# One list schedule for all engines, built groups by turns in two places of PSUM, and the dense unit of 181 nodes first

## The reference

```python
def gnn(features, src, dst, edge_weight, W, b):
    msgs = features[src] * edge_weight[:, None]
    agg = jax.ops.segment_sum(msgs, dst, num_segments=3125, indices_are_sorted=True)
    return jnp.einsum('ni,oi->no', agg, W) + b

def ffn(x, ...):                      # 4 experts, the best 2 of them kept
    all_out = experts_mlp(x, eW1, eb1, eW2, eb2, eW3, eb3)   # 256 -> 128 -> 64 -> 256 each
    shared = shared_mlp(x, sW1, sb1, sW2, sb2, sW3, sb3)     # 256 -> 256 -> 128 -> 256
    gates = softmax(x @ gW + gb)
    topv, topi = top_k(gates, 2)
    topw = softmax(topv)
    return shared + sum(take(all_out, topi) * topw)

x = x + gnn(layernorm(x), src, dst, edge_weight, W, b)
x = x + ffn(layernorm(x))
```

## Time and profile before

| | us |
|---|---|
| Median of 3 runs | 450.18 (449.88 to 450.70) |
| Profiled execution | 449.92 |
| Its span | 448.2 |
| TensorE matmuls busy | 361.6 (81%) |
| GpSimd busy | 311.4 (69%) |
| VectorE busy | 232.5 (52%) |
| ScalarE busy | 159.8 (36%) |

### The profile page before, as it was taken

One profiled execution on the slowest core, in us unless ns is written; L12 is line 12 of the kernel. 1 busy time (PEld: TensorE's weight loads), 2 busy tenths in 40 slices (PEclk: granted clock), 3 DMA queues, 4 the chain that ended last, 5 costly groups with the idle time before them and its releaser, 6 DMA issues.

```text
span 448.2 us, 7469 instructions
## 1 busy us (share of the span) xinstructions
PE 361.6 (81%) x2410; PEld 290.2 (65%) x2410; DVE 232.5 (52%) x905; ACT 159.8 (36%) x332; POOL 311.4 (69%) x319
## 2 busy tenths in 40 slices
PE   0004627979999989898999999998988999789785
PEld 0003325858878877776788876876676887468574
DVE  7899944753314555777352337535840523624242
ACT  1545162522412544352332234443411322322362
POOL 7776777777777777777777777777777777773000
PEclk9999958899999999999999999999988999899999
DMA  6994754344435334444333433434343334332000
GB/s 184 371 343 108 218 115 100 93 107 109 107 107 127 99 108 119 122 105 119 103 101 104 129 107 94 130 95 129 105 118 107 101 106 125 108 101 87 9 9 29
DMA packets 48962, 53.31 MB, mean 119 GB/s; under 512 B 27819, under 2 KB 38810, under 8 KB 48922
## 3 DMA queue, kind: packets, MB, share of 16 engines
q0 software_dynamic: 14784, 40.39, 30.9%
q1 hardware_dynamic: 30442, 9.14, 8.7%
q10 hardware_dynamic: 3696, 3.28, 2.1%
HBM read 46.30 MB, written 6.48 MB: 118 GB/s over the span
## 4 chain that ended last, share of the span: by engine, by line
POOL 52%; issue 19%; PE 18%; DMA 4%; DVE 3%; SPq 1%; ACT 1%; POOLq 0%; DVEq 0%
POOL rows L662 52%; PE hid_ps L973 5%; DMA x_sb<-in_x 3%; PE agg_ps L922 3%; PE window_ps L877 2%; PE tok_ps L1014 2%; PE agg_ps L938 1%; PE tok_ps L1012 1%; PE agg_ps L895 1%; SPq L543 1%; PE hid_ps L982 1%; PE tok_ps L1015 1%; PE mid_ps L959 1%; PE hid_ps L986 1%; PE tok_ps L1003 1%
## 5 line engine op out<-in xcount | busy, mean ns | idle before, releaser
L662 POOL DMA_INDIRECT rows<-normalised_rows,src_all x284 | 286.0, 1007 | 88.9 <-issue 88.6
L922 PE MATMUL agg_ps<-dense,xn_all 128*128 128x256 f32 (+1 forms) x300 | 67.2, 372 | 1.1 <-ACT dense L737 1.1
L910 PE MATMUL build_ps<-high_node,low_1h 128*128 128x125 f32 x282 | 44.0, 304 | 29.8 <-ACT dense L737 18.8
L910 PEld LDWEIGHTS build_ps<-high_node,low_1h 128*128 128x128 f32 x282 | 39.8, 215 | 34.5 <-issue 20.6
L922 PEld LDWEIGHTS agg_ps<-dense,xn_all 128*128 128x128 f32 x300 | 55.0, 198 | 8.3 <-issue 2.0
L877 PE MATMUL window_ps<-rows,select 128*32 128x256 f32 x616 | 42.7, 410 | 5.0 <-DMA rows<-normalised_rows,src_all 4.8
L973 PE MATMUL hid_ps<-xt,ew_sb 128*128 128x256 f32 (+2 forms) x224 | 46.5, 360 | 0.0
L785 ACT ACTIVATE h<-hid_ps,b_sb 128x256 f32<-128x256 f32 (+2 forms) x84 | 32.7, 442 | 32.6 <-PE hid_ps L973 32.6
L973 PEld LDWEIGHTS hid_ps<-xt,ew_sb 128*128 128x128 f32 x224 | 39.3, 195 | 5.7 <-issue 1.6
L1379 DVE TENSOR_TENSOR x<-agg_ps,x_sb 128x512 f32<-128x512 f32 (+1 forms) x14 | 8.8, 632 | 64.4 <-issue 44.5
L737 ACT ACTIVATE dense<-build_ps 128x500 f32<-128x500 f32 (+1 forms) x36 | 22.9, 635 | 42.6 <-PE build_ps L910 41.8
(11 more groups left out here) (143 smaller groups left out, 540.3 us busy)
## 6 DMA issues: line engine op xcount, KB each, us to landing
rows<-normalised_rows,src_all POOLq DMA_INDIRECT x284, 2.8
x_sb<-in_x SPq DMA_DIRECT2D x6, 512.0 KB, 10.3
normalised_rows<-xn_all ACTq DMA_DIRECT2D x6, 512.0 KB, 6.9
out<-y SPq DMA_DIRECT2D x10, 256.0 KB
records<-in_rec SPq DMA_DIRECT2D x144, 1.5 KB
ew_sb<-in_ew SPq DMA_DIRECT2D x1, 512.0 KB
out<-y SPq DMA_DIRECT2D x4, 128.0 KB
rows<-in_x,src_first POOLq DMA_INDIRECT x24, 3.8
```

The source lines that it names most:

```text
L662: pool.indirect_dma_start(rows[:, b % RING * BATCH + pos, :], None, table[:, :], bass.IndirectOffsetOnAxis(ap=src_all[:, c:c + 1], axis=0) ...
L910: last = pe.matmul(build_ps[:, j * width:(j + 1) * width], low_1h[:, k % RING, j, :], high_node[:, k % RING, j, :, :].rearrange("p h n -> ...
L922: last = pe.matmul(dense_ps[:, k * PAIR:k * PAIR + tok], xn_all[:, h, k * P:(k + 1) * P], dense[:, h, 0:tok], start=(h == 0 and k == 0), s ...
```

## The change

The change has five parts.

- `schedule()` is written anew. It keeps a clock for each of PE, ACT, DVE and SP, holds for every step of a unit its engine, duration and what it needs, and always gives the next place to the engine and step that can begin first; among what can begin within 0.2 us the lower rank goes first. What it needs of a gather is worked out from the ring (`land`).
- Groups are built by turns: even ones into `build_ps`, odd ones into the second bank of `agg_ps`, which is the place of the dense products (`dense_ps`). `build` k waits for the copy of group k - 2. An odd group of D1 or D2 also waits until the sums of the dense unit before have been copied out.
- The dense unit of 181 nodes is now D0, and the two of 256 nodes are D1 and D2.
- The raw rows of batch 1 are normalised in two steps of six rows, and their square root is a step of its own. The counts for the windows of D1 and D2 are done by one step `counted`.
- SyncE's record loads and stores stand in the order that the schedule gives.

The order of units was G0 G1 G2 D0 G3 G4 G5 D1 G6 G7 G8 D2 G9 G10, and is now G0 G1 G2 D0 G3 G4 D1 G5 G6 G7 D2 G8 G9 G10. The instructions are otherwise the same, with the same shapes, but that ScalarE has two table loads fewer.

```diff
-DENSE = [Unit("D", 0, 19, 2, PAIR), Unit("D", 1, 21, 2, PAIR), Unit("D", 2, 23, 2, P + TAIL)]
+DENSE = [Unit("D", 0, 23, 2, P + TAIL), Unit("D", 1, 19, 2, PAIR), Unit("D", 2, 21, 2, PAIR)]
...
+PARTS, OPEN, BANKS = 2, 2, 2
+NEAR, BEHIND, HURRY, FIRST = 0.2, 1.6, 3.0, -0.5
+COUNT_BEHIND, STATS_BEHIND = 6, 3
...
+    def land(b):
+        if b not in gathered:
+            if b < RAW_BATCHES:
+                gathered[b] = 20.0
+            else:
+                before = gathered_end(b - 1)
+                freed = at("batch", b - RING) if b >= RING else 0.0
+                if before is None or freed is None:
+                    return None
+                gathered[b] = max(before, freed) + 1.275 * batch_size(b)
+        return gathered[b]
...
+            ("act", "std", 1.6, lambda: needs(of("residual"))),
...
+            ("act", "ex", 1.5, lambda: needs(of("route"))),
...
+            ("act", "gex", 0.2, lambda: None if of("rank") is None else of("rank") - 0.9),
...
+        best = None
+        for engine in free:
+            found = [(max(r, free[engine]), rank, item, took) for r, rank, item, took in offers(engine)]
+            if found:
+                begin = min(f[0] for f in found)
+                pick = min((f for f in found if f[0] <= begin + NEAR), key=lambda f: (f[1], f[0]))
+                if best is None or pick[0] < best[1][0]:
+                    best = engine, pick
+        engine, (begin, _, item, took) = best
+        free[engine] = begin + took
+        done[item] = free[engine] + lag[engine]
+        order[engine].append(item)
         name, of = item[0], item[1]
...
+        def built_in(k):
+
+            return dense_ps if k % BANKS else build_ps
...
-                if k:
-                    pe.wait_ge(s_build_copied, k)
+                if k >= BANKS:
+                    pe.wait_ge(s_build_copied, k - BANKS + 1)
+                if v and k % BANKS:
+                    pe.wait_ge(s_copied["D"], v)
...
```

More of the change, by code:

```diff
@@ L103, in block_of @@
     return [(w, t0 // BLOCK) for w, t0, _ in BLOCKS].index((v, g * GROUP // BLOCK))
+PARTS, OPEN, BANKS = 2, 2, 2
+NEAR, BEHIND, HURRY, FIRST = 0.2, 1.6, 3.0, -0.5
+COUNT_BEHIND, STATS_BEHIND = 6, 3
 def schedule():
-    orders = {n: [] for n in ("pe", "act", "dve")}
-    done, units = {}, []
-    now, clock, gather = 32.0, 33.5, {}
-    batches = [(b,) for b in range(N_BATCHES)]
-    for b, i in [(b, i) for b in range(N_BATCHES) for i in range(QUADS)]:
-        if b >= RAW_BATCHES:
-            clock += 1.3 * len(quad(b, i))
-        gather[b] = clock + 2.8 if b >= RAW_BATCHES else (38.0, 51.0)[b]
@@ L118, in schedule @@
-    pieces = []
-    for v in range(len(DENSE)):
-        pieces += [("build", k) for k, (w, g) in enumerate(GROUPS) if w == v]
-        pieces += [("mult", v, h) for h in range(HI)]
-    names = ("lin", "turn", "l1a", "l1b", "l1c", "l2", "tgt", "spr", "l3")
-    waiting = {"G": list(GATHERED), "D": list(DENSE)}
-    open_units, merged = [], []
-    def put(engine, at, *item):
-        orders[engine].append((at, len(orders[engine]), item))
-    put("dve", 39.0, "rowstats", 1)
-    put("act", 44.0, "rows", 1)
@@ L185, in cost @@
-    def cost(item):
-        name = item[0]
-        if name in ("batch", "build"):
-            return 1.65 if name == "batch" else 1.13
-        u = DENSE[item[1]] if name == "mult" else item[1]
-        half = u.tok / PAIR
-        return {"mult": 0.86 * half, "merge": 0.48 * len(batches_of(u)), "lin": 1.86 * half,
-                "turn": 0.65 * half, "l1a": 2.75 * half, "l1b": 1.9 * half, "l1c": 1.9 * half,
-                "l2": 2.1 * half, "tgt": 0.35, "spr": 1.0 * half, "l3": 3.8 * half}[name]
@@ L274, in schedule @@
-    return {e: [item for _, _, item in sorted(o, key=lambda r: r[:2])] for e, o in orders.items()}, units
+    lag = {"pe": 0.35, "act": 0.12, "dve": 0.12, "sp": 2.2}
+    free = {"pe": 34.0, "act": 36.0, "dve": 33.0, "sp": 36.5}
+    order = {e: [] for e in free}
+    done, units, left = {("load", 0): 26.0}, [], {}
+    open_units = []
+    waiting = {"G": list(GATHERED), "D": list(DENSE)}
+    nxt = {"batch": 0, "windows": 0, "select": 0, "place": 0, "build": 0, "built": 0, "onehot": 0,
+           "records": 0, "mult": 0, "load": 1, "store": 0}
@@ new lines, in offers @@
+    def offers(engine):
+        out = fixed(engine)
+        for rank, u in enumerate(open_units):
+            for step in left[u]:
+                if step[0] == engine:
+                    ready = step[3]()
+                    if ready is not None:
+                        out.append((ready, -1.0 if u == GATHERED[-1] else rank * (BEHIND if engine == "pe" else 0.1),
+                                    (step[1], u), step[2]))
+                    if engine == "pe" or step[1] not in ("h1a", "h1b", "h1", "ex", "gex"):
+                        break
+        return out
@@ L277 @@
+    return order, units
 ORDER, UNITS = schedule()
```

322 lines of the change are left out of this document (174 added, 148 removed).

## The result

The changed kernel takes 443.91 us at the median of four runs (442.39 to 445.65), the kernel before 450.03 (four runs, 449.60 to 450.70). The ratio is 0.9864, its 95% interval 0.9825 to 0.9903. Forecast was 444.0 with a range of 440.6 to 449.0. The profiled execution took 444.12 us, with 1.72 around its span.

A forecast was written before the change was run, and what follows sets the result against it. Bound by GpSimd's gathers with TensorE nearly abreast: rows landing 410.4, arrears 0.8 and tail 30.8 give a 442.0 us span; 1.72 around it makes 443.7, adjusted to 444.0 for the median run. Range 440.6 to 449.0.

The forecast's parts named there:

- rows of batch 25 are there: Landing of the last gathered batch: the gathers wait for nobody, so its rows stay at 410.4 us.
- arrears at batch 25: How late TensorE starts batch 25 after its rows are there: 0.8 us, against 4.4 before.
- tail: From the start of batch 25 to the span's end: 30.8 us against 33.5, bounds 28.2 to 33.5.
- (b): Slower: TensorE waits ahead of batches bring the low clock; time is lost once batch 25 is 7 us late; chance 0.12.
- 2.6 us come back: In the tail, ScalarE's two table loads around G10's square root delay layer 2 of G9 from 10.8 to 13.4.
- The arrears and the middle: Up to batch 20, TensorE's savings (7.5 us of build waits, 4 at the start) become waiting and gain nothing.
- 3.5 us are arrears, 2.7 the tail: Split of the forecast gain of 6.2 us: about 3.5 from batch 25 starting earlier, 2.7 from a shorter tail.
- The start: Batch 1 runs at 58 us, not 68.99, and batch 3 near 72.4; TensorE is 4 to 5 us ahead at 76.
- Batches 20 to 25: TensorE's work between batches, 8.5 to 14.6 us, fits between gather arrivals; batch 25 starts at 411.2, 3.5 us earlier.
- (a): Arrears stay: batch 25 starts at 414.7 as before, only the tail gains, 447.5 us; chance 0.18.
- (c): Gathers themselves change, up to 17.5 us lying in long ones: no gain taken, 2 us either way; within the forecast's 0.62.
- (d): The loads hide or the clock stays up everywhere, and batch 25 starts at once: 440.6 us; chance 0.08.

The follow-up runs named there:

- the kernel with the late start: Whole change, but VectorE's shifts for raw batch 1 moved behind one-hot group number 6, so batch 1 starts 9 us later: 446.36 us, ratio 0.9913.
- the root moved: Whole change, but G10's square root moved behind G9's last layer 1 block on ScalarE, its normalisation behind G9's mixing weights on VectorE: 442.66 us, ratio 0.9848.
- The kernel with the dense unit last: Whole change, but the dense unit of 181 nodes is last of the three again: 449.99 us, ratio 1.0013 to the kernel before.
- one place with 181 nodes first: Whole change, but all groups built in one place (BANKS = 1), the 181-node unit still first: 444.27 us, ratio 0.9824.

## Why the prediction was right, step by step

**The sum.** Each term against its measurement:

| term | forecast | measured |
|---|---|---|
| rows of batch 25 are there | 410.4 | 408.76 |
| arrears at batch 25 | 0.8 | 0.43 |
| tail | 30.8 | 33.21 |
| span | 442.0 | 442.4 |

The span is right to 0.4 us, but by errors against each other: gathers 1.64 and arrears 0.37 earlier, the tail 2.4 longer. That it fits so closely is luck.

**The term mis-sized: the tail.** Its chain came as worked out up to layer 2 of G9, at +13.30 (forecast +13.4), behind a wait of 2.61 for ScalarE (forecast 2.6), and the turn of G10 at +15.63 (+15.5). Then the first layer of G10 ran at the lower of TensorE's two levels, 1.2 GHz: the block at 426.84 took 2.06 us, where the same one in the kernel with the late start, at 431.09, took 1.14. The granted clock from 426.84 to 429.00 is 0.50. Layer 2 of G10 came at +24.65, forecast +22.4. The late-start kernel has the same instructions and the same wait (2.62), kept the high clock and needed +21.99 and a tail of 30.33. The windows of both behind batch 25:

```profile
409.20:442.40 33.20, 25.06 (x158) 21.09 (x158) 11.00 (x52) 11.85 (x31) 0.00 (x0) 0.90 0.06 18
```

```profile
414.50:444.80 30.30, 22.35 (x158) 18.63 (x158) 10.95 (x52) 12.00 (x31) 0.00 (x0) 0.99 0.06 20
```

158 records of TensorE take 25.06 us in the one and 22.35 in the other, at granted clocks of 0.90 and 0.99. So the forecast of 30.8 is the tail at the high clock. The two tails are 2.9 us apart, and 2.7 of these lie ahead of layer 2 of G10, where the clock fell. The prediction knew of this: it read it behind batch 22 and used it in rival (b) ahead of batch 25. It left it out of the tail, where it put a wait of 2.6 us itself. Of four profiled executions with this tail three show the fall (the whole change twice, the new schedule alone) and one does not (late start); with the root moved, where the waits are 1.56 and 1.03, it did not fall either. What decides it for the same instructions is open.

**The two loads.** The step "2.6 us come back" had the size of the wait right and half of its cause wrong. With the loads away from `gex` the wait is still 1.56, since VectorE's gate of G9 stands behind G10's residual. The rule of the Trainium skill, "ScalarE: Activation LUTs", section "What ACT_TABLE_LOAD costs", would have a drain of 1.38 us with each switch. In the tail of the kernel after, the root begins 0.02 us after its load has ended (418.30 + 1.28, 419.60) and `gex` 0.01 after its own (419.91 + 1.28, 421.20), and the second load begins 0.02 after the root has ended (419.60 + 0.29). The trace shows no drain on either side, so the prediction was right to keep 1.28.

**The arrears and the middle.** As forecast, nothing that TensorE wins in the middle reaches the end: the builds' waits are gone, and 22.5 us of waiting for rows stand in their place. The kernel with two places and nothing else (0.9996 [0.9962, 1.0030]) shows by itself that fewer waits of builds do not reach the end. But "3.5 us are arrears, 2.7 the tail" took the two as separate. The kernel with the dense unit last has no arrears and no gain. Only their sum is bound by the order of units: 37.2 to 37.9 where G8 goes ahead of D2, 30.4 to 33.6 where D2 goes ahead of G8, 27.7 to 31.0 where G8 is done too. Within the last two groups it is mostly the clock; the 32.8 of one place with 181 nodes first are at the high clock (0.99), with arrears of 1.31 and 24.2 us of work.

**The start.** Batch 1 at 58.18 (forecast 58), batch 2 at 61.51, batch 3 at 72.09 (72.4), after a wait of 1.17 for the counts, in the kernel after:

```profile
58.18 2.79 PE L933 MATMUL window_ps<-rows,select 128*32 128x256 f32 x24 [11.01 <-issue]
61.51 1.51 PE L933 MATMUL window_ps<-rows,select 128*32 128x256 f32 x24 [0.54 <-issue]
...
68.98 0.43 PE L899 MATMUL window_ps<-smaller_n,ones 128*128 128x56 f32 x2 [1.17 <-DVE smaller_n L1233]
72.09 2.79 PE L933 MATMUL window_ps<-rows,select 128*32 128x256 f32 x24 [2.68 <-DMA rows<-normalised_rows,src_all]
```

For batch 3 the number was right by luck. The prediction had its rows at 70.3 and the begins of the windows as the last thing to come. In fact its last gather starts at 69.16, so its rows are there at 71.96, and they end its wait of 2.68; the begins were ready at 71.4. What the early start brings is not to be seen at batch 25, as forecast and as the late start shows.

**Batches 20 to 25.** The sums between the batches fitted: batch 20 had waited 0.36, batch 22 1.71, batch 24 0.58 for rows. The forecast of waits inside the chains and 0.8 of arrears was on the safe side by 0.4.

**The rivals.** (a) and (b) did not come: arrears are 0.43. (c) did, by 1.6 us on the good side, within the 2 put on it. (d) came in half: batch 25 started at once, but the wait for ScalarE came (2.61), and the clock did not stay up. The Trainium skill, "SBUF — State Buffer", section "SBUF: two separate sides", which stood behind (c), says that VectorE, in some modes or with two inputs in SBUF, and GpSimd lock each other out of a shared port, and that descriptors of GpSimd's DMAs then come late. The gathers agree as far as they show it: 26 of 52 beside the wide products are long, 14 of the other 232. The form with one SBUF tensor and a column as scalar did not help (277.9 to 281.2). That does not speak against the rule, which names modes beside the two inputs; in which mode this form ran no run shows.

## What to carry to other kernels

Where one stream (here the gathers) never waits, split the span into its landing, the arrears of the engine behind it, and the tail, and judge a change of order by the sum of the last two: arrears alone can be bought with work put off. What counts is how much work still stands behind the last arrival. Here it became less by one line in which the smallest dense unit comes first, since D2 was then opened one or two units earlier; the rest of the change brought nothing on top. Waits removed in the middle turned into waits for the stream or for another engine here (22.5 us for rows in the whole change). Where a tail has a wait of 2 to 3 us on TensorE, give it two prices, at the high clock and at the low, since the same instructions took 30.3 and 33.2 us.

## What the runs showed of the hardware that was not expected

The clock fell behind a wait of 2.61 us in one kernel and not behind one of 2.62 in another with the same instructions on TensorE around it. With the old schedule and the 181 nodes first, it fell for 10 us behind a wait of 2.20 (the first-layer block 2.05 us) and with two places besides, behind a wait of 2.17, for some 4 (the same block 1.14).

The last of the same 284 gathers started between 405.96 and 411.28 in ten kernels, with medians of 946 to 949 ns in all of them. This spread of 5.3 us is nearly as large as the whole gain (6.1). In the last set of runs, on another chip, the same programs took 640 to 675 us at the median, with stops on several engines that no row of the profile explains.
